# The ninth power in an angular attention kernel: three squarings on ScalarE and one product on VectorE, in place of two squares and two products

## The chip, the cores and the metric

The kernel runs on one core of a Trainium2 chip. The metric is the device time of one execution in microseconds (us). Engines are named as in the profile: PE (TensorE), ACT (ScalarE), DVE (VectorE), POOL (GpSimd), SP (SyncE, which here only starts DMAs).

## The reference, cut to what matters

The program is four residual layers over 4096 tokens of width 128: an angular attention, a mixture of experts, a linear attention, and the mixture of experts again. The change touches the first layer alone:

```
Q = _l2_normalize(x)
K = _l2_normalize(k_weight)
s = jnp.clip(jnp.einsum('nh,ih->ni', Q, K), -1.0 + 1e-06, 1.0 - 1e-06)
B = jnp.power(1.0 - jnp.arccos(s) / jnp.pi, TAU)      # TAU = 9
X = jnp.einsum('ni,ih->nh', B, q_weight)
X = _l2_normalize(X) + bias
```

There are 512 keys, so B has 4096 x 512 values. Up to a factor that the normalisation of X removes, B is the ninth power of (arctan(z) + pi/2), with z = s / sqrt(1 - s^2).

## The kernel before, in words

The program is written engine by engine. Each engine has its own list of instructions, in an order fixed in the code; the engines meet only at semaphores. A helper, `steps(engine, count, unroll, parts)`, writes a software pipeline: each part has a lag, and step s does part(s - lag) for every part in the order given. Where at least two rounds of `unroll` steps fit between the first steps and the last, `steps` turns them into a loop of the engine; else all is written out straight (lines 67 to 94).

The 4096 tokens are 8 groups (NG) of 512. For the scores each group is split in two halves of the keys, so there are 16 units (NA), numbered n; a unit is a tile of 128 x 1024 fp32. First come the scores: PE multiplies (line 815), ACT squares and takes the inverse root (lines 624, 628), DVE multiplies (`tangent`, line 1182) and leaves z of all 16 units in SBUF (`big`). When all are done, ACT loads the table that has the arctangent, and the stage of the ninth power begins. I call it the power stage. For unit n, in slot k = n % 4 of the buffers RR and SC:

- `angle` (ACT, line 647): RR = arctan(z). It waits until `ninth` of unit n - 4 has freed the slot.
- `angle_square` (ACT, line 651): SC = (RR + pi/2)^2.
- `third` (DVE, line 1232): RR = (RR + pi/2) * SC, the third power.
- `sixth` (ACT, line 655): SC = RR^2, the sixth power.
- `ninth` (DVE, line 1239): PB = RR * SC.

After every second unit a group g is whole:

- `value` (PE, line 835): PB times q_weight into the PSUM tile PC, 32 matmuls in the trace. It waits for `ninth`, and for `add_values` of group g - 2, which frees its PC bank.
- `value_squares` (ACT, line 665): four sums of squares of 128 columns, for the norm.
- `x_scale` (POOL, lines 539 and 503): the inverse root of the norm.
- `add_values` (DVE, line 1250): adds the scaled rows to X, and takes the statistics of the next layer norm (line 1036).

On ACT a step is `angle(n)`, `sixth(n-2)`, `angle_square(n)`, and on every second step `value_squares` of the group whose last unit is n - 5. On DVE a step is `ninth(n-3)`, `third(n)`, and on every second step `add_values` for unit n - 7. When all eight groups are in, `statistics(1)` on DVE combines the statistics of all tokens (line 1060 on); no token of the mixture of experts can start before. POOL writes a memset of 7 us (line 548) after its last `x_scale`.

Of the kernel before, what the change touches and what calls it, by code (L numbers as in the profile page):

```python
# [16 lines left out]
ALU = mybir.AluOpType  # L17
ACT = mybir.ActivationFunctionType
# [18 lines left out]
HALF_PI = float(np.pi / 2)  # L37
# [10 lines left out]
def wait(engine, semaphore, value):  # L48

    if isinstance(value, int) and value <= 0:  # L50
        return
    engine.wait_ge(semaphore, value)
# [8 lines left out]
def steps(engine, count, unroll, parts, table=None):  # L61

    most = max(lag for lag, _ in parts)

    first = unroll * (1 + -(-max(0, most - 1) // unroll)) if unroll > 2 else 2 * -(-(most + 1) // 2)
    loops = max(0, (count - first) // unroll)  # L70

    def straight(s):
        for lag, part in parts:
            u = s - lag
            if 0 <= u < count:
                part(u, u // unroll, u % unroll, *(table(u, 1) if table else ()))

    if loops < 2:
        for s in range(count + most):
            straight(s)  # L80
        return
    for s in range(first):
        straight(s)
    with engine.Fori(0, loops) as i:
        known = {}
        for k in range(unroll):
            for lag, part in parts:
                c = (k - lag) % unroll
                h = i + (first + k - lag - c) // unroll
                if table and k - lag not in known:  # L90
                    known[k - lag] = table(i * unroll + (first + k - lag), 1)[0]
                part(h * unroll + c, h, c, *([known[k - lag]] if table else ()))
    for s in range(first + loops * unroll, count + most):
        straight(s)


def build(nc, x_in, ln_w, ln_b, k_w, q_w, a_bias, w_qkv, w_out, gate_w, gate_b,
# [12 lines left out]
    NA = 2 * NG  # L110
# [9 lines left out]
    with ctx:  # L120
        def sb(name, shape, dt=F32):
            return ctx.enter_context(nc.sbuf_tensor(name, shape, dt))

        def sem(name):
            return ctx.enter_context(nc.semaphore(name))
# [54 lines left out]
        PB = sb("PB", [P, 2, HB, GT])  # L180
# [6 lines left out]
        SC, RR = sb("SC", [P, 4, 1024]), sb("RR", [P, 4, 1024])  # L187
# [113 lines left out]
        def read(ring, part, slot, n):  # L301
# [7 lines left out]
            bn_done stat_step var_ready root_ready xn_done  # L309
            yt_a ysq_a norm_a qt_a bias_added  # L310
            s_ready u_ready r_ready
            at_ready sq_ready p3_ready s6_ready p9_ready o_ready ss_ready rx_ready
            xh_ready xl_ready xt_ready gate_ready route_step pm_ready counts_ready places_ready
            gap_ready th_ready routed_out_ready rows_ready
            cb_parts cbt_ready b2_loaded b2_steps scattered0 scattered1 scattered2 scattered3
# [9 lines left out]
        s = {n: sem(n) for n in names}  # L325
# [13 lines left out]
        def angles_done(engine, n, h, k):  # L339

            engine.wait_ge(a_read[k % 2], read("A", "score", k % 2, 2 * h + k // 2))
# [14 lines left out]
        def table_values(engine_type, table, stride):  # L356

            def values(u, n):
                _, found = nc.values_load_multi_w_load_instructions(
                    table[0:1, bass.ds(u, n)], [engine_type], min_val=0, max_val=(E - 1) * stride,  # L360
                    skip_runtime_bounds_check_because="the table's experts are clamped")
                return found
            return values
# [223 lines left out]
        def _(act):  # L587
# [62 lines left out]
                act.wait_ge(s["at_ready"], n + 1)  # L650
                act.activation(SC[:, k, :], RR[:, k, :], ACT.Square, bias=halfpi[:]).then_inc(s["sq_ready"], 1)  # L651

            def sixth(n, h, k):
                act.wait_ge(s["p3_ready"], n + 1)
                act.activation(SC[:, k, :], RR[:, k, :], ACT.Square).then_inc(s["s6_ready"], 1)

            def value_squares(n, h, k):
                if k % 2 == 0:
# [10 lines left out]
            act.wait_ge(s["k_squares"], HB)  # L669
            for n in (NA - 2, NA - 1):  # L670
                angles_done(act, n, n // 4, n % 4)
            for n in range(NA + 5):
                for lag, part in ((0, angle), (2, sixth), (0, angle_square), (5, value_squares)):
                    u = n - lag
                    if 0 <= u < NA:
                        part(u, u // 4, u % 4)
# [350 lines left out]
        def _(dve):  # L1027
# [199 lines left out]

            bias_parts()

            def third(n, h, k):  # L1230
                dve.wait_ge(s["sq_ready"], n + 1)
                dve.scalar_tensor_tensor(RR[:, k, :], RR[:, k, :], HALF_PI, SC[:, k, :], ALU.add,
                                         ALU.mult).then_inc(s["p3_ready"], 1)

            def ninth(n, h, k):
                g, slot = 2 * h + k // 2, k // 2
                dve.wait_ge(s["s6_ready"], n + 1)
                wait(dve, s["o_ready"], g - 1)
                dve.tensor_tensor(PB[:, slot, 2 * (k % 2):2 * (k % 2) + 2, :].rearrange("p b t -> p (b t)"),  # L1239
                                  RR[:, k, :], SC[:, k, :], ALU.mult).then_inc(s["p9_ready"], 1)  # L1240

            def add_values(n, h, k):
                if k % 2 == 0:
# [11 lines left out]
                bn(1, g)  # L1255


            steps(dve, NA, 4, [(3, ninth), (0, third), (7, add_values)])
            statistics(1)

            for layer in range(2):
                sp_ = f"shared{layer}"
                if layer:
                    part = "linear"
# [336 lines left out]
```

## Time and profile before

| what | us |
|---|---|
| median of 3 runs | 924.19 (915.52 to 929.87) |
| profiled execution, device time | 923.3 |
| its span in the trace | 921.4 |
| power stage: ACT's table load to the last statistics on DVE | 110.8 to 182.5 |
| PE busy, whole span | 562.0 (61%) |
| DVE busy | 598.9 (65%) |
| ACT busy | 382.5 (42%) |
| POOL busy | 389.8 (42%) |

All times of single instructions come from the one profiled execution. In the timeline the first column is the start, the second the time until the end; on ACT and DVE the end of an instruction overlaps the start of the next by about a tenth of a microsecond, so the cost of an instruction in a full queue is the distance between two starts, not its length.

### The profile page before, as it was taken

The numbers are of one execution on the slowest core, as the hardware profiler recorded it, in microseconds if no ns is written. First come the engines' busy times: TensorE is split into PE (matmuls) and PEld (weight loads), VectorE is DVE, ScalarE is ACT, GpSimd is POOL, SyncE is SP. The second block draws the span as 40 slices with busy tenths as digits, with TensorE's granted clock in tenths as the row PEclk, the third lists the DMA queues.
The fourth block names the chain that finished last, engine by engine and source line by source line (L and its number), as shares of the span: only waits on it lengthen the run. The fifth ranks groups of instructions, "written<-read, shape, count | busy, mean of one in ns | idle before, by whom it ended". The sixth has DMA issues, their size and how long they took to land.

```text
span 921.4 us, 17336 instructions
## 1 busy us (share of the span) xinstructions
PE 562.0 (61%) x5073; PEld 412.8 (45%) x5074; DVE 598.9 (65%) x1367; ACT 382.5 (42%) x685; POOL 389.8 (42%) x360
## 2 busy tenths in 40 slices
PE   0647546544038698888780488442083998887850
PEld 0223246422025376766660377321052676776640
DVE  5899768785268266766674667782473666666644
ACT  1454898452103254545450244451021454644520
POOL 3096012316748306566572000037476026664650
PEclk9977967955559799999995699765586999999985
DMA  9100000001101523332315000001012223232207
GB/s 288 48 0 0 1 0 1 0 1 37 51 26 51 122 43 76 68 72 68 70 45 194 9 1 1 0 18 53 27 44 76 53 42 80 62 77 61 69 36 279
DMA packets 90830, 51.83 MB, mean 56 GB/s; under 512 B 71482, under 2 KB 79892, under 8 KB 90772
## 3 DMA queue, kind: packets, MB, share of 16 engines
q1 hardware_dynamic: 81556, 32.07, 14.3%
q0 software_dynamic: 9216, 19.02, 6.3%
q8 instruction: 32, 0.52, 0.2%
q14 instruction: 26, 0.21, 0.1%
HBM read 16.28 MB, written 24.30 MB: 44 GB/s over the span
## 4 chain that ended last, share of the span: by engine, by line
PE 42%; DVE 21%; issue 19%; ACT 9%; another core or an unknown queue 3%; DMA 3%; POOL 1%; ACTq 0%; DVEq 0%; SPq 0%; POOLq 0%
PE PC L1016 5%; PE PC L1018 4%; PE PC L1017 4%; PE PA L1000 2%; PE PC L979 2%; PE PA L1002 2%; PE PA L1001 2%; DVE PB L1086 2%; PE PC L981 2%; PE PA L849 2%; PE PC L980 2%; PE PA L815 2%; DMA RR<-expert_results 2%; ACT SC L651 1%
## 5 line engine op out<-in xcount | busy, mean ns | idle before, releaser
L579 POOL DMA_INDIRECT expert_results<-RR,DG x160 | 181.3, 1133 | 188.2 <-DVE RR L1548 148.7
L567 POOL DMA_INDIRECT routed_rows<-big,SLQ x128 | 139.6, 1091 | 196.0 <-DVE SLQ L1409 158.8
L771 ACT ACTIVATE SC<-PA,B1T,scl 128x256 f32<-128x256 f32 x216 | 104.0, 568 | 110.3 <-remote 64.0
L1016 PE MATMUL PC<-W2H,big 128*128 x640 | 124.7, 224 | 14.6 <-issue 8.6
L1017 PE MATMUL PC<-W2H,big 128*128 x640 | 122.9, 222 | 7.0 <-issue 7.0
L1018 PE MATMUL PC<-W2L,big 128*128 x640 | 122.8, 222 | 7.1 <-issue 6.9
L1539 DVE SCALAR_TENSOR_TENSOR big<-SC,scl,big 128x1024 f16<-128x1024 f32 x80 | 102.8, 1285 | 2.8
L1548 DVE SCALAR_TENSOR_TENSOR RR<-PC,scl,DG 128x256 f32<-128x256 f32 x80 | 38.4, 481 | 87.3 <-remote 77.2
L730 ACT ACTIVATE SC<-PA,B1T,scl 128x512 f32<-128x512 f32 x64 | 45.0, 776 | 102.1 <-PE PA L937 45.2
L1016 PEld LDWEIGHTS PC<-W2H,big 128*128 128x128 f16 x640 | 63.1, 99 | 36.6 <-issue 28.4
L1536 DVE TENSOR_SCALAR big<-SC,scl 128x1024 f16<-128x1024 f32 x80 | 61.8, 772 | 12.7 <-ACT SC L771 10.6
L1018 PEld LDWEIGHTS PC<-W2L,big 128*128 128x128 f16 x640 | 63.2, 99 | 12.1 <-issue 10.9
L979 PE MATMUL PC<-W2H,big 128*128 128x128 f16 x256 | 52.0, 234 | 26.2 <-DVE big L1447 17.2
L1017 PEld LDWEIGHTS PC<-W2H,big 128*128 128x128 f16 x640 | 63.7, 100 | 9.0 <-issue 8.5
L771 ACT ACTIVATE SC<-PB,B1T,scl 128x256 f32<-128x256 f32 x104 | 50.4, 569 | 34.2 <-remote 17.3
L1000 PE MATMUL PA<-big,W1H 128*128 128x256 f16 x216 | 60.2, 279 | 3.3 <-issue 3.0
L1002 PE MATMUL PA<-big,W1L 128*128 128x256 f16 x216 | 59.7, 276 | 3.4 <-issue 2.9
L1001 PE MATMUL PA<-big,W1H 128*128 128x256 f16 x216 | 59.8, 277 | 2.0 <-issue 2.0
L835 PE MATMUL PC<-QW,PB 128*128 128x128 f32 x256 | 37.1, 314 | 33.1 <-DVE PB L1239 17.5
L981 PE MATMUL PC<-W2H,big 128*128 128x128 f16 x256 | 51.8, 233 | 8.2 <-issue 8.1
L980 PE MATMUL PC<-W2L,big 128*128 128x128 f16 x256 | 51.8, 233 | 6.7 <-issue 6.7
L835 PEld LDWEIGHTS PC<-QW,PB 128*128 128x128 f32 x256 | 35.6, 227 | 35.3 <-DVE PB L1239 18.5
(245 smaller groups left out, 1358.7 us busy)
## 6 DMA issues: line engine op xcount, KB each, us to landing
RR<-expert_results SPq DMA_DIRECT2D x16, 512.0 KB, 4.6
routed_rows<-big SPq DMA_DIRECT2D x24, 130.0 KB
expert_results<-RR,DG POOLq DMA_INDIRECT x160
X<-n_L_attn_a_hidden_states SPq DMA_DIRECT2D x2, 1024.0 KB, 6.7
big<-in_L_ffn_w SPq DMA_DIRECT2D x1, 2048.0 KB, 8.8
routed_rows<-big,SLQ POOLq DMA_INDIRECT x128
out_x<-X SPq DMA_DIRECT2D x8, 256.0 KB, 5.2
big<-routed_rows SPq DMA_TRANSPOSE x80
```

The source lines that it names most:

```text
L567: pool.indirect_dma_start(routed, bass.IndirectOffsetOnAxis(ap=SLQ[:, slot, t, c:c + 1], axis=0), XHL[:, slot, t, c, :].bitcast(I32), None ...
L579: pool.indirect_dma_start(results, bass.IndirectOffsetOnAxis(ap=DG[:, k, r, 0:1], axis=0), YT[:, k, r, :], None).then_inc(result_stored[k] ...
L771: ins = act.activation(HF[:, k % 3, b * RU:(b + 1) * RU], up_out(k, b), ACT.Gelu, scale=INV1, bias=B1T[:, bass.ds(b1_at + b, 1)])
L835: last = pe.matmul(PC[slot][:, t * D:(t + 1) * D], PB[:, slot, b, t * P:(t + 1) * P], QW[:, b, :], start=(b == 0), stop=(b == HB - 1))
L979: pe.matmul(o, hh, W2H[:, c:c + P], start=(b == 0), stop=False)
L1000: pe.matmul(o, W1H[:, at], xh, start=True, stop=False)
L1001: pe.matmul(o, W1H[:, at], xl, start=False, stop=False)
L1002: last = pe.matmul(o, W1L[:, at], xh, start=False, stop=True)
L1016: pe.matmul(o, hh, W2H[:, at], start=(b == 0), stop=False)
L1017: pe.matmul(o, hl, W2H[:, at], start=False, stop=False)
L1018: last = pe.matmul(o, hh, W2L[:, at], start=False, stop=(b == HB - 1))
L1539: dve.scalar_tensor_tensor(HL3[:, k % 3, :], HF[:, k % 3, 0:HB * RU], SH, HH3[:, k % 3, :], ALU.mult, ALU.subtract).then_inc(s["rhl_ready" ...
```

## The change

The ninth power is built as ((a^2)^2)^2 * a, with a = arctan(z) + pi/2. `third` and `sixth` go. Two squarings in place, `fourth` and `eighth`, come on ACT, and `ninth` takes a and a^8 in one DVE instruction that also adds pi/2. `value_squares` and `add_values` lag by 3 steps and no longer by 5 and 7.

```
-            def sixth(n, h, k):
-                act.wait_ge(s["p3_ready"], n + 1)
-                act.activation(SC[:, k, :], RR[:, k, :], ACT.Square).then_inc(s["s6_ready"], 1)
+            def fourth(n, h, k):
+                act.wait_ge(s["sq_ready"], n + 1)
+                act.activation(SC[:, k, :], SC[:, k, :], ACT.Square).then_inc(s["p4_ready"], 1)
+
+            def eighth(n, h, k):
+                act.wait_ge(s["p4_ready"], n + 1)
+                act.activation(SC[:, k, :], SC[:, k, :], ACT.Square).then_inc(s["p8_ready"], 1)
...
-            for n in range(NA + 5):
-                for lag, part in ((0, angle), (2, sixth), (0, angle_square), (5, value_squares)):
+            for n in range(NA + 3):
+                for lag, part in ((0, angle), (1, fourth), (0, angle_square), (1, eighth), (3, value_squares)):
...
-            def third(n, h, k):
-                dve.wait_ge(s["sq_ready"], n + 1)
-                dve.scalar_tensor_tensor(RR[:, k, :], RR[:, k, :], HALF_PI, SC[:, k, :], ALU.add,
-                                         ALU.mult).then_inc(s["p3_ready"], 1)
-
             def ninth(n, h, k):
                 g, slot = 2 * h + k // 2, k // 2
-                dve.wait_ge(s["s6_ready"], n + 1)
+                dve.wait_ge(s["p8_ready"], n + 1)
                 wait(dve, s["o_ready"], g - 1)
-                dve.tensor_tensor(PB[:, slot, 2 * (k % 2):2 * (k % 2) + 2, :].rearrange("p b t -> p (b t)"),
-                                  RR[:, k, :], SC[:, k, :], ALU.mult).then_inc(s["p9_ready"], 1)
+                dve.scalar_tensor_tensor(PB[:, slot, 2 * (k % 2):2 * (k % 2) + 2, :].rearrange("p b t -> p (b t)"),
+                                         RR[:, k, :], HALF_PI, SC[:, k, :], ALU.add,
+                                         ALU.mult).then_inc(s["p9_ready"], 1)
...
-            steps(dve, NA, 4, [(3, ninth), (0, third), (7, add_values)])
+            steps(dve, NA, 4, [(0, ninth), (3, add_values)])
```

How the order changes. ACT, at the end of the power stage, before: L647 is `angle`, L655 `sixth`, L651 `angle_square`, L665 `value_squares`.

```order
L647 ACTIVATE RR<-big 128x1024
L655 ACTIVATE SC<-RR 128x1024
L651 ACTIVATE SC<-RR,halfpi 128x1024
L665 ACTIVATE junk,SS<-PC 128x128 x4
L647 ACTIVATE RR<-big 128x1024
L655 ACTIVATE SC<-RR 128x1024
L651 ACTIVATE SC<-RR,halfpi 128x1024
L655 ACTIVATE SC<-RR 128x1024
L665 ACTIVATE junk,SS<-PC 128x128 x4
L655 ACTIVATE SC<-RR 128x1024
L665 ACTIVATE junk,SS<-PC 128x128 x8
```

The same place in the changed kernel, where L655 is `fourth`, L659 `eighth`, and L669 `value_squares`:

```order
L647 ACTIVATE RR<-big 128x1024
L655 ACTIVATE SC<-SC 128x1024
L651 ACTIVATE SC<-RR,halfpi 128x1024
L659 ACTIVATE SC<-SC 128x1024
L669 ACTIVATE junk,SS<-PC 128x128 x4
L647 ACTIVATE RR<-big 128x1024
L655 ACTIVATE SC<-SC 128x1024
L651 ACTIVATE SC<-RR,halfpi 128x1024
L659 ACTIVATE SC<-SC 128x1024
L655 ACTIVATE SC<-SC 128x1024
L659 ACTIVATE SC<-SC 128x1024
L669 ACTIVATE junk,SS<-PC 128x128 x8
```

A step has four large passes and no longer three. The last `fourth` and `eighth` stand next to each other, and no `value_squares` is left between the last two units.

DVE, at the end of the power stage, before: L1239 is `ninth`, L1232 `third`, L1250 and L1036 `add_values`.

```order
L1232 SCALAR_TENSOR_TENSOR RR<-RR,SC 128x1024
L1239 TENSOR_TENSOR PB<-RR,SC 128x1024
L1250 SCALAR_TENSOR_TENSOR X<-PC,RX,X 128x128 x4
L1036 BN_STATS BN<-X 128x6 x4
L1239 TENSOR_TENSOR PB<-RR,SC 128x1024 x2
L1250 SCALAR_TENSOR_TENSOR X<-PC,RX,X 128x128 x4
L1036 BN_STATS BN<-X 128x6 x4
```

The same place in the changed kernel: the second half of the loop's body, from the `ninth` (L1238) of its third unit on, and what stands behind the loop (L1250 and L1040 are `add_values`; ISA and REGISTER_ALU rows compute addresses and waits).

```order
L1238 SCALAR_TENSOR_TENSOR PB<-RR,SC 128x1024
L1246 ISA
L1250 ISA
L1250 SCALAR_TENSOR_TENSOR X<-PC,RX,X 128x128
...
L1040 BN_STATS BN<-X 128x6
L1236 REGISTER_ALU
L1238 SCALAR_TENSOR_TENSOR PB<-RR,SC 128x1024
L84 REGISTER_ALU
L84 COMPARE_AND_BRANCH
L1250 SCALAR_TENSOR_TENSOR X<-PC,RX,X 128x128 x4
L1040 BN_STATS BN<-X 128x6 x4
```

DVE's steps 8 to 15 are now a loop of two rounds, which they were not before; the largest lag fell from 7 to 3, and with it the steps that must be written out. In each round, and so in the last one too, an `add_values` stands between the third unit's `ninth` and the fourth's.

## Rows read from the trace of the kernel before

**Rows 1.** The page, part 1: busy time, share of the span, instructions.

```profile
PE 562.0 (61%) x5073; PEld 412.8 (45%) x5074; DVE 598.9 (65%) x1367; ACT 382.5 (42%) x685; POOL 389.8 (42%) x360
```

**Rows 2.** Busy time by stretch: the power stage; all after the next statistics.

```profile
core 0: us, PE busy (x) PEld busy (x) DVE busy (x) ACT busy (x) POOL busy (x), PEclk, DMA share, GB/s
110.80:182.50 71.70, 37.11 (x256) 35.60 (x256) 55.50 (x106) 58.79 (x114) 14.40 (x17) 0.79 0.00 0
189.00:921.40 732.40, 467.04 (x4696) 352.51 (x4696) 447.71 (x1098) 270.63 (x502) 321.08 (x289) 0.82 0.23 60
```

**Rows 3.** Who waited for whom, 110.8 to 182.5: us, times, longest us.

```profile
PE PC L835 <- DVE X L1250: 15.7, 6, 5.9
DVE RR L1232 <- ACT SC L651: 11.2, 13, 1.7
ACT junk L665 <- PE PC L835: 9.3, 5, 3.5
ACT RR L647 <- DVE PB L1239: 1.0, 2, 0.5
```

**Rows 4.** Timeline of ACT, power stage: start, length, instruction [idle before, releaser].

```profile
112.11 1.06 ACT L647 ACTIVATE RR<-big 128x1024 f32<-128x1024 f32 x1
113.20 1.15 ACT L651 ACTIVATE SC<-RR,halfpi 128x1024 f32<-128x1024 f32 x1
114.25 1.04 ACT L647 ACTIVATE RR<-big 128x1024 f32<-128x1024 f32 x1
...
119.31 1.04 ACT L647 ACTIVATE RR<-big 128x1024 f32<-128x1024 f32 x1
120.26 1.04 ACT L655 ACTIVATE SC<-RR 128x1024 f32<-128x1024 f32 x1
121.20 1.13 ACT L651 ACTIVATE SC<-RR,halfpi 128x1024 f32<-128x1024 f32 x1
122.24 1.04 ACT L647 ACTIVATE RR<-big 128x1024 f32<-128x1024 f32 x1
...
131.04 0.26 ACT L665 ACTIVATE junk<-PC 128x128 f32<-128x128 f32 x1
...
132.04 1.06 ACT L647 ACTIVATE RR<-big 128x1024 f32<-128x1024 f32 x1
...
168.75 1.07 ACT L655 ACTIVATE SC<-RR 128x1024 f32<-128x1024 f32 x1
173.27 0.28 ACT L665 ACTIVATE junk<-PC 128x128 f32<-128x128 f32 x1 [3.45 <-PE PC L835]
...
177.58 0.28 ACT L665 ACTIVATE junk<-PC 128x128 f32<-128x128 f32 x1 [3.17 <-PE PC L835]
```

**Rows 5.** Timeline of ACT in the score stage: a pass in place.

```profile
96.71 1.06 ACT L628 ACTIVATE SC<-SC 128x1024 f32<-128x1024 f32 x1
```

**Rows 6.** Timeline of DVE, end of the power stage.

```profile
167.08 1.22 DVE L1239 TENSOR_TENSOR PB<-RR,SC 128x1024 f32<-128x1024 f32 x1
168.22 1.12 DVE L1250 SCALAR_TENSOR_TENSOR X<-PC,RX,X 128x128 f32<-128x128 f32 x4
169.49 0.87 DVE L1036 BATCH_NORM_STATS2 BN<-X 128x6 f32<-128x128 f32 x4
170.27 2.34 DVE L1239 TENSOR_TENSOR PB<-RR,SC 128x1024 f32<-128x1024 f32 x2
...
181.65 0.87 DVE L1036 BATCH_NORM_STATS2 BN<-X 128x6 f32<-128x128 f32 x4
```

**Rows 7.** Timeline of PE, power stage: four of the eight products with q_weight.

```profile
140.37 6.59 PE L835 MATMUL PC<-QW,PB 128*128 128x128 f32 x32 [5.88 <-DVE X L1250]
147.88 3.84 PE L835 MATMUL PC<-QW,PB 128*128 128x128 f32 x32 [0.93 <-DVE X L1250]
156.33 5.47 PE L835 MATMUL PC<-QW,PB 128*128 128x128 f32 x32 [4.62 <-DVE X L1250]
173.71 3.84 PE L835 MATMUL PC<-QW,PB 128*128 128x128 f32 x32 [0.47 <-DVE X L1250]
```

**Rows 8.** Timeline of DVE: statistics in a loop, in the linear attention.

```profile
546.17 0.86 DVE L1036 BATCH_NORM_STATS2 BN<-X  x4
```

**Rows 9.** Groups by line and shape, 110.8 to 182.5: count, busy us, mean ns.

```profile
L1232 DVE SCALAR_TENSOR_TENSOR RR<-RR,SC 128x1024 f32<-128x1024 f32 x16 | 19.6, 1224 | 11.2 <-ACT SC L651 11.2
L1239 DVE TENSOR_TENSOR PB<-RR,SC 128x1024 f32<-128x1024 f32 x16 | 19.4, 1215 | 0.0
```

More of the change, by code:

```diff
@@ L311, in build @@
             s_ready u_ready r_ready
-            at_ready sq_ready p3_ready s6_ready p9_ready o_ready ss_ready rx_ready
+            at_ready sq_ready p4_ready p8_ready p9_ready o_ready ss_ready rx_ready
             xh_ready xl_ready xt_ready gate_ready route_step pm_ready counts_ready places_ready
```

## The prediction

> **What bounds the kernel now.** I read the page first and then asked it only for the place of the change. The page gives DVE as the busiest engine of the compute engines that the change touches, 65% against 42% for ACT [rows 1]. That is a mean over the whole program. The busy time by stretch turns it round for the power stage: in its 71.7 us ACT is busy 58.8 us (82%), DVE 55.5 us (77%), PE 37.1 us [rows 2]. No engine is full, so the waits have to say who holds whom. DVE's `third` waits for ACT in 13 of 16 units, 11.2 us in all; PE waits for `add_values` of DVE in 6 of 8 groups, 15.7 us, since the PC bank comes free late; and ACT waits for that PE in five `value_squares`, 9.3 us, and twice for a slot, 1.0 us [rows 3]. Two of those five waits, 3.45 and 3.17 us, lie behind the last `sixth`, in the drain of the pipeline [rows 4]; so 9.3 - 3.45 - 3.17 + 1.0 = 3.7 us is what ACT loses while it still has large passes to do. The reader is to see: ACT is nearly the bound here, with 3.7 us to spare up to its last pass, and DVE is second.
>
> Outside the stage nothing overlaps it. It begins when all scores are done, and it ends in statistics over all tokens, which everything later needs; no DMA runs in it (share 0.00 [rows 2]). A shift of its end is a shift of the kernel's end, unless later stages happen to run otherwise.
>
> **The change part by part.** I follow ACT from its second `angle` at 114.25 [rows 4], which stands at the same place in both orders (arctangent, square, arctangent), and whose inputs the change doesn't touch.
>
> *One large pass more for each unit on ACT.* The three starts 119.31, 120.26, 121.20, and the next `angle` at 122.24, give 0.95 us for the arctangent, 0.94 for the plain square, 1.04 for the square with the bias from SBUF, 2.93 us for a step [rows 4]. The new step has a second plain square, so 2.93 + 0.95 = 3.88 us. 15 steps (n = 1 to 15) are 58.2 us. Between them lie six `value_squares` (groups 0 to 5) of 132.04 - 131.04 = 1.00 us each, 6.0 us. The last `fourth` starts at 114.25 + 58.2 + 6.0 = 178.45. The last `eighth` stands directly behind it and needs its result; the distance of two such dependent neighbours is 113.20 - 112.11 = 1.09 us [rows 4]. It starts at 179.54 and ends 1.04 us later, at 180.58. Before, the last `sixth` ended at 168.75 + 1.07 = 169.82. So ACT is 10.8 us later. As a check: 16 passes of 0.95 are 15.2 us, less the 3.7 us of waits that vanish is 11.5; the 0.7 us between the two is what the first and the last steps of the old pipeline lost.
>
> Passes in place were not seen in this stage. In the score stage one takes 1.06 us from and to SC [rows 5], the same as a pass between two tiles. Below 0.94 us there is no reason for one. Above, the bound is that each of the 32 shows its result's latency, 1.09 in place of 0.95: 31 x 0.14 = 4.3 us more. I take nothing, since between `angle_square` and `fourth`, and between `fourth` and `eighth`, another pass lies, as lay between `angle` and `angle_square` before, which show 0.94 there.
>
> *DVE loses a pass and gets a loop.* `third` goes, 16 x 1.14 us of queue (168.22 - 167.08 is the distance behind a large product [rows 6]), about 18 us; `ninth` becomes the form of `third`, 1.224 against 1.215 us [rows 9], 0.01 us. None of the 18 us is on ACT's path: it is worth nothing beyond the 3.7 us of waits above. The loop of two rounds adds address and branch work. Statistics inside a loop take 0.86 us for four [rows 8], those written out 0.87 [rows 6], so the body costs nothing that rows show; a round's branch and the first entry are not in a row, and I allow up to 1 us. It is covered: for a group of 2 x 3.88 + 1.00 = 8.76 us DVE has 2 x 1.14 + 1.27 + 0.78 = 4.3 us of work, so 4.4 us are free, except at the very end.
>
> The Trainium skill (ScalarE: Activation LUTs, Rules for kernel authors) says that products belong on VectorE and not on ScalarE, for a speed up to three times higher in bf16. In fp32 the rows here show 1.14 us for a product on DVE and 0.95 us for a square on ACT, so its reason doesn't hold, but its direction does, because ACT is the fuller engine of this stage.
>
> *Who waits for whom in the middle.* From the end of `eighth` of a group's second unit to its `value_squares` ACT does two steps and one other `value_squares`, 8.7 us. In that time fit `ninth` 1.2 us, the matmuls 3.84 us with the clock high up to 6.59 us after a long idle stretch [rows 7], and two hand-overs of 0.05: 5.1 to 7.9 us. There is room, 0.8 us in the worst case, so ACT shouldn't wait. `add_values` needs only `value_squares` of the step before it, and `value` finds its bank free. `angle` waits for a `ninth` three steps back. PE will be idle 8.76 - 3.84 = 4.9 us in each group when fast; in the rows an idle of 4.6 and 5.9 us is followed by 5.47 and 6.59 us of matmuls, one of 0.93 or 0.47 us by 3.84 [rows 7]. So PE will be slower here, unseen.
>
> *The drain.* Two things stand ahead of the last product. The last-but-one `ninth` starts when its `eighth` ends, at 178.45 + 0.10 = 178.55. Behind it DVE has `add_values` of group 5 and only then the last `ninth`: 1.14 + 1.27 + 0.78 = 3.19 us [rows 6], so 181.74, which is 1.2 us later than the last `eighth` would allow. It ends at 182.96 and PE starts at 183.0. Then come the last 32 matmuls. Bounds are 3.84 and 6.59 us; PE will have been idle for about 8.0 less its own burst, 1.5 to 4.2 us, between the idles of the fast and the slow rows, so I take the middle, 5.2 us. From the end of the matmuls to the last statistics took (181.65 + 0.87) - (173.71 + 3.84) = 4.97 us [rows 6, 7], and the same instructions stand there. Sum: 183.0 + 5.2 + 4.97 = 193.2, against 182.5 before: **10.7 us later**. Of these, ACT is 10.8, the wait of the drain 183.0 - 180.58 against 173.71 - 169.82 is -1.5, and the slower matmuls are +1.4. With both bounds of the matmuls: 9.3 to 12.1 us.
>
> The profiled execution took 923.3 us for a span of 921.4. 923.3 + 10.7 = 934.0 us. It lay 0.9 us under the median of the runs shown, well inside their 14 us, so I leave it there.
>
> **The rivals.**
>
> *Dependent passes show their latency.* The queue of ACT now has three passes of each unit that hang on one another. If each costs 1.09 us, the 4.3 us above come on top: 938.3. For it speaks the pair at 112.11 and 113.20; against it that `angle_square` two places behind its `angle` shows nothing.
>
> *ACT stalls for PE in every group.* If the matmuls stay slow in all groups and DVE's loop delays `ninth`, the 7.9 us of the chain pass the 8.7 us of cover. It decides from 0.8 us of delay on, and each further 1 us costs 1 us in each of 7 groups. With the allowance of 1 us for the loop in each round and matmuls of twice 3.84 = 7.7 us (not seen in a row) the chain is 10.0 us, 1.3 too long, 7 x 1.3 = 9 us more: 943. Against it: the loop has only two rounds.
>
> *The other side: DVE is the bound, and the change is no loss.* The page shows DVE fullest [rows 1], the ring of PC banks runs over DVE's queue, and the change takes 18 us from it and shortens the lags. If ACT's passes could be packed more closely than 0.95 us the ring would set the pace; it would gain the 3.7 us, and the drain 1.5 more: 923.3 - 5.2 = 918. Its condition is that the 16 new passes (15.2 us) cost less than 15.2 - 10.7 = 4.5 us, 0.28 us each. A square of 1024 columns at 0.94 us in 16 rows speaks plainly against it. The Trainium skill (Perfetto Trace Analysis, Identifying the Most-Contended Engine, and Optimizing Scalar/DVE Operations) says to relieve the engine with the highest occupancy first, and that work moved from a saturated DVE to ScalarE may help; it also says to look within a regime. The occupancy of the whole span supports this rival, that of the stage doesn't.
>
> *The loss is given back later.* From 189 us on the clock of PE is 0.82 on the mean [rows 2]; between levels of 0.5 and 1.0 this is 36% of 732 us, 264 us, at the low one. A shifted start changes what falls into them. To win back 10.7 us, 21 us of these 264 would have to turn fast on the chain. That is 924 or less. The spread of the runs before, 14 us, says that such sizes occur, in both directions.
>
> **How the numbers follow.** Chances: the forecast 0.62, latency of dependent passes 0.13, stalls in every group 0.07, given back later 0.14, DVE as the bound 0.04. The forecast's own range with the bounds of matmuls and loop and half of the runs' spread is 928 to 940. The full range takes in the latency rival and most of the give-back: 923 to 943. About 2% (18.5 us) is what a measurement of this kernel can tell from no change; the forecast, 1.1% slower, lies within. Slower by over 2% needs the stalls or two rivals together, 0.08; faster by over 2% needs the DVE rival and more, 0.02; within 2% 0.90.
>
> **What would show it.** ACT's starts in the stage should be 0.95 apart with no idle ahead of `value_squares` up to the last `eighth`, which ends near 180.6. DVE's busy time in the stage falls by some 19 us and it waits for `eighth` in nearly every unit. The last `ninth` starts 1.2 us after the last `eighth` ended, behind `add_values`. Matmuls of a group take 4 to 6.6 us. The last statistics end near 193, and all behind it is shifted by that. The prediction is wrong if plain squares in place are 1.09 apart, if ACT waits for PE ahead of `value_squares`, or if the stage is 10 us longer and the kernel isn't.

## The result, and where the time went

| | median us | runs |
|---|---|---|
| kernel before | 922.43 | 4 (915.52 to 929.87) |
| changed kernel | 944.24 | 4 (942.88 to 949.85) |

The ratio is 1.0235 with a 95% interval of 1.018 to 1.029: 21.8 us slower, twice the 10.7 us that were forecast, and 1.2 us outside the range. I compare the profiled execution (944.69 us, span 942.5) with that of before (923.3 and 921.4).

The timeline of ACT in the changed kernel, at the start of the power stage, in a middle step and at the end:

```profile
111.53 1.06 ACT L647 ACTIVATE RR<-big 128x1024 f32<-128x1024 f32 x1
112.62 1.15 ACT L651 ACTIVATE SC<-RR,halfpi 128x1024 f32<-128x1024 f32 x1
113.67 1.04 ACT L647 ACTIVATE RR<-big 128x1024 f32<-128x1024 f32 x1
114.62 1.04 ACT L655 ACTIVATE SC<-SC 128x1024 f32<-128x1024 f32 x1
115.56 1.13 ACT L651 ACTIVATE SC<-RR,halfpi 128x1024 f32<-128x1024 f32 x1
116.60 1.04 ACT L659 ACTIVATE SC<-SC 128x1024 f32<-128x1024 f32 x1
117.55 1.04 ACT L647 ACTIVATE RR<-big 128x1024 f32<-128x1024 f32 x1
...
177.82 1.12 ACT L655 ACTIVATE SC<-SC 128x1024 f32<-128x1024 f32 x1
178.97 1.06 ACT L659 ACTIVATE SC<-SC 128x1024 f32<-128x1024 f32 x1
...
186.54 0.28 ACT L669 ACTIVATE junk<-PC 128x128 f32<-128x128 f32 x1 [5.40 <-PE PC L839]
```

These answer to [rows 4]. The step is 117.55 - 113.67 = 3.88 us, as worked out. The squares in place stand 0.94 and 0.95 us before the next start. There is no bracket with idle time between the first pass and the last: ACT is full. The last `eighth` ends at 180.03, 68.5 us after the first arctangent; before it was 169.82 - 112.11 = 57.7. ACT is 10.8 us later, the number of the forecast.

The timeline of DVE over the drain:

```profile
178.03 1.23 DVE L1238 SCALAR_TENSOR_TENSOR PB<-RR,SC 128x1024 f32<-128x1024 f32 x1 [3.66 <-ACT SC L659]
179.17 1.12 DVE L1250 SCALAR_TENSOR_TENSOR X<-PC,RX,X 128x128 f32 x4
180.54 0.87 DVE L1040 BATCH_NORM_STATS2 BN<-X  x4 [0.25 <-DVE X L1250]
181.33 1.21 DVE L1238 SCALAR_TENSOR_TENSOR PB<-RR,SC 128x1024 f32<-128x1024 f32 x1
...
190.60 0.87 DVE L1040 BATCH_NORM_STATS2 BN<-X 128x6 f32<-128x128 f32 x4
```

The last `ninth` starts at 181.33, 1.3 us after its input was there, behind `add_values` of group 5; the same pieces before are in [rows 6]. The timeline of PE, against [rows 7]:

```profile
156.97 5.70 PE L839 MATMUL PC<-QW,PB 128*128 128x128 f32 x32 [4.94 <-DVE PB L1238]
165.73 3.83 PE L839 MATMUL PC<-QW,PB 128*128 128x128 f32 x32 [3.06 <-DVE PB L1238]
174.50 5.46 PE L839 MATMUL PC<-QW,PB 128*128 128x128 f32 x32 [4.94 <-DVE PB L1238]
182.67 3.83 PE L839 MATMUL PC<-QW,PB 128*128 128x128 f32 x32 [2.71 <-DVE PB L1238]
```

All eight starts hang on `ninth`, none on the PC bank any more. The last product took 3.83 us, the lower bound. The busy time by stretch says the same of the whole stage, against [rows 2]:

```profile
110.20:191.47 81.27, 38.12 (x256) 36.62 (x256) 37.50 (x90) 73.25 (x130) 13.29 (x17) 0.79 0.00 0
```

(Columns: stretch, its length, busy us of PE, PE's weight loads, DVE, ACT, POOL, the granted clock.) DVE fell from 55.5 to 37.5 us, ACT rose from 58.8 to 73.3. From the first arctangent to the first statistics over all tokens the stage took 79.98 us against 70.44: 9.5 us longer.

So a little under half of the loss lies here and the rest does not. With the last product at its lower bound, the forecast for the stage was 9.3 us.

I divide what is left at the first DVE operation behind the root (R), the first load of routed rows (X0, X1), the first load of results (Y0, Y1), and the first statistics behind the linear attention (M):

| us | before | changed |
|---|---|---|
| R to X0: gates, shared expert, scatter, layer 0 | 131.4 | 137.6 |
| X0 to Y0: routed experts | 172.8 | 173.4 |
| Y0 to M: linear attention | 93.7 | 93.7 |
| M to X1: gates, shared expert, layer 1 | 131.7 | 140.8 |
| X1 to Y1 | 182.5 | 178.0 |
| Y1 to end | 20.2 | 21.0 |
| R to end | 732.3 | 744.5 |

12.2 us more. The two stages with the shared expert, whose code the change doesn't touch, are 6.2 and 9.1 us longer, 15.3 in all, and the second pass of the routed experts is 4.5 us shorter. What PE shows there: one line of the shared expert's product (L980 before, L984 in the changed kernel), its durations and what it waited for, in layer 0. First before:

```profile
L980 PE MATMUL PC<-W2L,big x128: 216/219/314, 268.7 to 335.3; 128*128 128x128 f16 x128
  issue: 5.7, 8
```

and the changed kernel:

```profile
L984 PE MATMUL PC<-W2L,big x128: 216/219/314, 277.7 to 351.5; 128*128 128x128 f16 x128
  issue: 7.8, 11
```

(Shortest, median and longest duration in ns, first and last start.) The product starts as late behind R in both, 79.6 and 79.7 us, and in layer 1 as late behind M, 81.9 and 82.2 us. So the stages grow behind its start: up to X0 from 51.8 to 57.8 us, up to X1 from 49.8 to 58.7. The same 128 matmuls spread over 73.8 us in place of 66.6. PE sits idle for "issue", which is time in which nothing that the profile shows holds it. In the changed kernel the timeline has it in pieces of half a microsecond, ahead of single matmuls:

```profile
290.86 0.22 PE L985 MATMUL PC<-W2H,big 128*128 128x128 f16 x1 [0.39 <-issue]
291.61 0.22 PE L984 MATMUL PC<-W2L,big 128*128 128x128 f16 x1 [0.47 <-issue]
292.32 0.23 PE L985 MATMUL PC<-W2H,big 128*128 128x128 f16 x1 [0.50 <-issue]
```

The mean granted clock is lower too: over the stretch of the shared expert 0.78 before (259 to 320 us) and 0.70 in the changed kernel (268 to 335 us). Which of the two comes first isn't shown. Such idle time stands in both kernels, and on this line it is only 2.1 us more in the changed one, which is less than the 7.2 us of the spread. Did the change cause this?

### The profile page after: what moved, and what is told of

Read it like the earlier page. It is cut to its first block, busy times and chain, and to the rows that moved or that the text cites. A ratio compares the mean times of both kernels' runs of the same rounds, so it can differ in the third digit from the quotient of the medians.

```text
span 942.5 us, 17389 instructions
## 1 busy us (share of the span) xinstructions
PE 571.8 (61%) x5073; PEld 419.7 (45%) x5074; DVE 580.7 (62%) x1351; ACT 397.3 (42%) x701; POOL 387.9 (41%) x360
## 4 chain that ended last, share of the span: by engine, by line
PE 41%; DVE 20%; issue 19%; ACT 12%; another core or an unknown queue 3%; DMA 3%; POOL 1%; DVEq 0%; SPq 0%; ACTq 0%; POOLq 0%
PE PC L1020 5%; PE PC L1022 4%; PE PC L1021 4%; PE PC L983 2%; PE PA L1004 2%; PE PA L1006 2%; PE PA L1005 2%; PE PC L985 2%; DVE PB L1090 2%; PE PC L984 2%; PE PA L853 2%; DMA RR<-expert_results 2%; ACT RR L647 2%; ACT SC L659 2%
## 5 line engine op out<-in xcount | busy, mean ns | idle before, releaser
L579 POOL DMA_INDIRECT expert_results<-RR,DG x160 | 183.9, 1150 | 200.0 <-DVE RR L1548 162.7
L567 POOL DMA_INDIRECT routed_rows<-big,SLQ x128 | 136.2, 1064 | 196.4 <-DVE SLQ L1409 159.2
L1020 PE MATMUL PC<-W2H,big 128*128 x640 | 127.3, 227 | 15.4 <-issue 10.8
L1022 PE MATMUL PC<-W2L,big 128*128 x640 | 125.3, 225 | 9.2 <-issue 9.2
L1021 PE MATMUL PC<-W2H,big 128*128 x640 | 125.9, 225 | 5.1 <-issue 4.9
L1020 PEld LDWEIGHTS PC<-W2H,big 128*128 128x128 f16 x640 | 64.0, 100 | 38.8 <-issue 30.7
L1021 PEld LDWEIGHTS PC<-W2H,big 128*128 128x128 f16 x640 | 64.8, 101 | 10.0 <-issue 9.5
L983 PE MATMUL PC<-W2H,big 128*128 128x128 f16 x256 | 53.4, 238 | 24.5 <-DVE big L1447 17.2
L839 PE MATMUL PC<-QW,PB 128*128 128x128 f32 x256 | 38.1, 319 | 41.7 <-DVE PB L1238 41.7
L985 PE MATMUL PC<-W2H,big 128*128 128x128 f16 x256 | 53.4, 238 | 8.9 <-issue 8.9
L984 PE MATMUL PC<-W2L,big 128*128 128x128 f16 x256 | 53.4, 237 | 8.6 <-issue 8.6
```

The lines of the kernel that those rows point to most:

```text
L567: pool.indirect_dma_start(routed, bass.IndirectOffsetOnAxis(ap=SLQ[:, slot, t, c:c + 1], axis=0), XHL[:, slot, t, c, :].bitcast(I32), None ...
L579: pool.indirect_dma_start(results, bass.IndirectOffsetOnAxis(ap=DG[:, k, r, 0:1], axis=0), YT[:, k, r, :], None).then_inc(result_stored[k] ...
L839: last = pe.matmul(PC[slot][:, t * D:(t + 1) * D], PB[:, slot, b, t * P:(t + 1) * P], QW[:, b, :], start=(b == 0), stop=(b == HB - 1))
L983: pe.matmul(o, hh, W2H[:, c:c + P], start=(b == 0), stop=False)
L1020: pe.matmul(o, hh, W2H[:, at], start=(b == 0), stop=False)
L1021: pe.matmul(o, hl, W2H[:, at], start=False, stop=False)
```

## The experiments

Theory SHIFT: the shared stages take a later start badly, by 12 us. Theory CODE or LOOP: the changed instruction lists do it, above all DVE's new loop. The third possibility is that it belonged to that measurement and not to the change. Fifteen runs were made in four sets, each on another chip (1, 7, 5 and 3) and beside the kernel before. The sets lie at different levels: the kernel before took 909.3, 912.7, 819.9 and 820.6 us. Whether a level belongs to the chip or to the occasion can't be told from them, and the chip of the first measurement is not on record. So times are compared within a set.

### Set 1: delay, loop, one pass fewer

**e1_shift9** puts nine chained passes on ACT ahead of the root of the next layer norm:

```
+                for i in range(passes):      # 9 in layer 0
+                    act.activation(SC[:, 0, :], SC[:, 0, :], ACT.Square, scale=1e-6).then_inc(s["spent"], 1)
+                    act.wait_ge(s["spent"], i + 1)
                 act.activation(EST[:], VA[:], ACT.Abs_reciprocal_sqrt).then_inc(s["root_ready"], 1)
```

> The kernel before, with nine squarings of a 128x1024 tile in a chain on ACT between the last variance and the root of the next layer norm: a pure delay of 9 x 1.09 = 9.8 us behind the power stage, the size of what the change adds ahead of it (9.5 us). Nothing else moves. Theory SHIFT (the 12 us that the change loses behind the stage come from when the experts' stages start against the clock's windows or the DMAs): the kernel loses about 9.8 + 12 = 22 us, 945. Theory CODE (they come from the changed code, DVE's new loop or the places where instruction fetches fall): it loses 9.8 us, 932.

Measured: 1.0148 (1.0094 to 1.0202), 13.5 us. The first statistics to the next root took 17.6 us and not 6.6: the delay is 11.0 us. The nine passes are 9.8 of it; the rest is a table load of 1.28 us on ACT, which now stands behind them. SHIFT wanted twice that; the interval, 8.5 to 18.4 us, holds the delay alone and excludes 22.

**e2_no_loop** writes DVE's part of the changed kernel out:

```
-            steps(dve, NA, 4, [(0, ninth), (3, add_values)])
+            for n in range(NA + 3):
+                for lag, part in ((0, ninth), (3, add_values)):
+                    u = n - lag
+                    if 0 <= u < NA:
+                        part(u, u // 4, u % 4)
```

> The changed kernel with DVE's ninth and add_values written out straight, as they stood before, and no loop. Theory LOOP (the new loop on DVE causes the 12 us behind the stage): about 932. Theory SHIFT: 944, as the changed kernel. Theory CODE in its wide form (where instruction fetches fall): between, since DVE's list is longer by some 20 instructions.

Measured: 1.0147 (1.01 to 1.0195), 13.4 us: between what LOOP and SHIFT wanted. Taken against the first measurement it spoke for LOOP, but the two come from different sets; e6 and e8 below compare them on one chip.

**e3_no_fourth** drops `fourth` (DVE then multiplies by a^4, so the output is the fifth power's):

```
-                for lag, part in ((0, angle), (1, fourth), (0, angle_square), (1, eighth), (3, value_squares)):
+                for lag, part in ((0, angle), (0, angle_square), (1, eighth), (3, value_squares)):
```

> The changed kernel without the fourth power: ninth multiplies by a^4, and the output is another one. ACT is back at three large passes a unit. The stage should shorten by 16 x 0.95 = 15.2 us plus the changed hand-overs, to about 66 us, 6 us shorter than before the change. Theory SHIFT: what lies behind the stage is that of before or otherwise, unlike the changed kernel's; 917 or so if it is that of before. Theory LOOP or CODE: the 12 us behind the stage stay, 929.

Measured: 1.0004 (0.9969 to 1.004). The stage took 70.3 us, not 66. My expectation forgot two things that the trace shows. First, `angle_square` now stands directly behind its `angle`:

```profile
146.01 1.04 ACT L647 ACTIVATE RR<-big 128x1024 f32<-128x1024 f32 x1
147.09 1.15 ACT L651 ACTIVATE SC<-RR,halfpi 128x1024 f32<-128x1024 f32 x1
148.14 1.04 ACT L655 ACTIVATE SC<-SC 128x1024 f32<-128x1024 f32 x1
```

1.08 and 1.05 us to the next start in place of 0.95 and 1.04. Second, with shorter steps ACT waits for PE again (0.60, 1.12 and 0.31 us ahead of three `value_squares` before the drain), and the drain stays as long as in the changed kernel. Still the run says one thing clearly: one pass a unit, 16 x 0.95 = 15.2 us of ACT, is the difference between the changed kernel and no loss, although its DVE has the loop and the 18 us of relief.

**e4_before_loop** gives the kernel before a DVE loop of two rounds, by one more argument of `steps`:

```
-            steps(dve, NA, 4, [(3, ninth), (0, third), (7, add_values)])
+            steps(dve, NA, 4, [(3, ninth), (0, third), (7, add_values)], first=8)
```

> The kernel before, with DVE's power stage as a loop of two rounds instead of written out; the same instructions in the same order. Theory LOOP: the stage keeps its length and the kernel loses 12 us behind it, 935. Theory SHIFT: no change, 922 to 924.

Measured: 0.9982 (0.9932 to 1.0032), the stage 70.5 us. The upper end of the interval is 3 us, far from LOOP's 12: a loop on DVE costs nothing that shows. LOOP is out, as far as the loop alone goes.

### Set 2: the changed kernel again, and a tighter pipeline

**e6_changed_again** is the changed kernel, **e7_before_traced** the kernel before, **e8_straight_again** the kernel of e2.

> The changed kernel itself, once more, beside the kernel before and the next runs. The straight version and the pure delay of nine passes each lost 1.5%, about 13 us, where the changed kernel was measured at 2.35%. If the changed kernel's extra is real and comes from DVE's loop: ratio 1.023 again. If it belonged to that measurement (the chip, or how the experts' stages fell): ratio 1.012 to 1.017, some 11 to 15 us, with the stage 9 to 12 us longer and nothing systematic behind it.

> The kernel before, unchanged, with a trace beside those of the other runs of this set. The ratio is 1.00. Its time from the root of the second layer norm to the end was 732.3 us in the first trace; SHIFT wants about 720 in this set, clearly less than in the changed kernel; the other theory wants the same length as in all the others of the set, give or take 5 us.

> The changed kernel without DVE's loop, beside the one with it. LOOP: 8 us faster than the changed kernel. Otherwise: the same within 0.5%.

Measured: the changed kernel 1.0119 (1.008 to 1.0157) over 6 runs against 23 of before, 923.03 against 912.69 us; the kernel before 0.9973 (0.994 to 1.0005); the straight version 1.0138 (1.0095 to 1.018). The loss of the changed kernel is 10.9 us here, and its interval does not touch that of the first measurement. Loop and no loop are the same. From R to the end the traces of sets 1 and 2 show 717.6 to 727.1 us in the seven runs other than e7, in no order of the start of R; e7 has 713.4. With R near 188 to 189 us (e3, e4, e7, e9) the mean is 719.7; with R at 197.6 to 200.5 us (e1, e2, e6, e8) it is 721.2. No effect of a late start of 12 us is in this.

**e9_tight** keeps the passes of the kernel before and shortens the lags:

```
-                for lag, part in ((0, angle), (2, sixth), (0, angle_square), (5, value_squares)):
+                for lag, part in ((0, angle), (2, sixth), (0, angle_square), (4, value_squares)):
...
-            steps(dve, NA, 4, [(3, ninth), (0, third), (7, add_values)])
+            steps(dve, NA, 4, [(2, ninth), (0, third), (5, add_values)])
```

> The passes of the kernel before (three on ACT, two on DVE), with ninth at lag 2, value_squares at lag 4 and add_values at lag 5 in place of 3, 5 and 7. ACT's waits (3.7 us) and one step of the drain go; the stage ends about 6 us earlier, near 176.5, and the kernel takes 6 us less than before (ratio 0.993). If what lies behind the stage depends on when it starts, the time can come out up to 10 us to either side of that.

Measured: 0.9994 (0.9966 to 1.0022); a miss. The stage took 70.2 us. The timeline of PE at the end:

```profile
159.12 3.83 PE L835 MATMUL PC<-QW,PB 128*128 128x128 f32 x32 [1.60 <-DVE PB L1239]
166.51 10.18 PE L835 MATMUL PC<-QW,PB 128*128 128x128 f32 x64 [3.55 <-DVE PB L1239]
```

The product of group 6 started at 166.51, behind a `ninth` that had itself stood behind `add_values` on DVE, and after 3.55 us of idle it and the last product took 10.2 us together. The step that failed is that ACT's 3.7 us of waits would go: up to its last `sixth` ACT still waited 3.2 us, 1.13, 0.72 and 0.38 us for PE ahead of three `value_squares` and 1.01 us for `third`. Why is argued and not tested: a group is 4 x 1.14 + 2.05 = 6.6 us of work on DVE and 6.9 us on ACT, so either engine is nearly full, and taking out one wait brings the next.

### Set 3: ACT's pass alone, and the order in the drain

**e10_fourth_pass** gives the kernel before a fourth large pass on ACT, a copy in place, and leaves DVE as it was:

```
+            def again(n, h, k):
+                act.wait_ge(s["spent"], n + 1)
+                act.activation(SC[:, k, :], SC[:, k, :], ACT.Copy).then_inc(s["s6_ready"], 1)
...
+                for lag, part in ((0, angle), (2, sixth), (0, angle_square), (2, again), (5, value_squares)):
```

> The kernel before with one more pass of 128x1024 on ACT for each unit, a copy of the sixth power onto itself behind angle_square; DVE keeps third and ninth. If ACT's pass alone makes the loss and DVE's relief is worth nothing: ACT's steps 3.88 us, the last large pass ends 10 to 11 us later than before, the stage is 9 to 12 us longer, the ratio 1.010 to 1.015, as the changed kernel. If DVE's relief gives something back in the changed kernel, this one is slower than the changed kernel by that, up to 3 us in the stage.

> The changed kernel a third time, for the ratio and for the spread behind the stage. By the chain worked out for the power stage: ratio 1.012 (1.008 to 1.016). If the first measurement's 1.0235 was the rule and the second the exception: 1.02 or more.

> The changed kernel with add_values ahead of ninth in DVE's steps, so that add_values of group 5 fills DVE's idle time before the last-but-one ninth and no longer stands between the last two. The last ninth starts when the last eighth ends, 1.1 us earlier against it than in the changed kernel (there 1.2 us behind the end of eighth), and the stage is 1.2 us shorter; in the time 0.1%, which can't be told.

> The kernel before, with a trace beside those of this set: power stage 70.5 us from the first arctangent to the statistics, and a time from the root of the layer norm to the end within 8 us of that of the changed kernel's in this set.

Measured: e10 1.0135 (1.0112 to 1.0157), e11 (the changed kernel) 1.0105 (1.0081 to 1.0129), e12 1.0092 (1.0064 to 1.012). e13 was a single execution. Traces: the stage took 70.2 us in e13 (before), 80.1 in e10 and 81.4 in e11. The last product of e10, then of e11:

```profile
182.51 3.84 PE L839 MATMUL PC<-QW,PB 128*128 128x128 f32 x32 [1.17 <-DVE X L1254]
```

```profile
182.72 5.25 PE L839 MATMUL PC<-QW,PB 128*128 128x128 f32 x32 [2.71 <-DVE PB L1238]
```

At equal products the two stages are alike within 0.1 us. **ACT's pass alone lengthens the stage by 9.9 us, as much as the changed kernel's is longer at equal products, and in the order that it has, the changed kernel gets nothing of it back for a DVE without `third` and with shorter lags.** The drains differ in kind, though: e10's last product waits 1.1 us behind its `ninth` for `add_values` to free the bank, and the changed kernel's last `ninth` waits 1.3 us behind `add_values`. By the medians e10 takes 2.2 us more than e11 (830.71 and 828.53; their intervals overlap). Its traced stage is not the longer one; the traces have the difference behind it, 631.1 against 629.0 us from R to the end.

e12 swaps two parts of the changed kernel:

```
-            steps(dve, NA, 4, [(0, ninth), (3, add_values)])
+            steps(dve, NA, 4, [(3, add_values), (0, ninth)])
```

Its ACT and DVE at the end:

```profile
178.62 1.06 ACT L659 ACTIVATE SC<-SC 128x1024 f32<-128x1024 f32 x1
```

```profile
177.72 1.21 DVE L1238 SCALAR_TENSOR_TENSOR PB<-RR,SC 128x1024 f32<-128x1024 f32 x1
179.71 1.22 DVE L1238 SCALAR_TENSOR_TENSOR PB<-RR,SC 128x1024 f32<-128x1024 f32 x1 [0.78 <-ACT SC L659]
```

The last `ninth` now starts 0.03 us after the last `eighth` ends (179.68). The stage is 78.7 us; against e11's 81.4, 1.4 of the 2.7 us are the product (3.83 against 5.25), and 1.3 the swap. The stage is also 1.4 us shorter than e10's, at equal products. By these single traces the changed kernel can get a little back in the drain, once DVE's order allows it; which part of that is the missing `third` and which the shorter lags is not shown. In the time it can't be told, as expected.

### Set 4: once more, against the pure delay

> The changed kernel once more. If this set's kernel before takes 915 to 930 us, as in the first measurement: a ratio of 1.02 or more says that the 12 us behind the power stage belong to the change in that condition, 1.008 to 1.016 that they were how its four runs fell. In a set of another level: 1.008 to 1.016.

> The kernel before with the pure delay of nine passes ahead of the root, 11 us measured. If what lies behind the stage takes a late start badly in this set, this one loses as much as the changed kernel, twice its delay; else 1.2 to 1.5%.

> The kernel before with its trace beside them: the length from the root to the end, and of the experts' stages in it, to hold against the changed kernel's. Without an effect of the change behind the stage the two agree within the 10 us that they scattered in the second set.

Measured: the changed kernel 1.0103 (1.0084 to 1.0121), 828.91 against 820.63 us; the pure delay 1.0143 (1.0128 to 1.0159); before 1.0001. R to end: 629.4, 629.4 and 631.1 us; in set 3 631.1 (e10), 629.0 (e11), 626.2 (e12) and 631.0 (e13). Here nothing behind the stage depends on the change or on the delay, within 5 us. In sets 3 and 4 the changed kernel's traced stage is 11.2 and 11.4 us longer, more than the loss in time of 8.6 and 8.5 us; the profiled executions (830.69 and 831.12 us) lay 2.2 us above their medians, and R to the end was 2.0 and 1.7 us shorter than before.

In these two sets the idle time on issue is gone. The same line as above, in layer 0, first e13 (before), then e11 (changed); neither answer has an issue row:

```profile
L980 PE MATMUL PC<-W2L,big x128: 219/219/314, 239.4 to 296.3; 128*128 128x128 f16 x128
```

```profile
L984 PE MATMUL PC<-W2L,big x128: 219/219/314, 250.9 to 309.0; 128*128 128x128 f16 x128
```

57 and 58 us, against 66.6 and 73.8 in the first measurement, and in set 2, e7 (before):

```profile
L980 PE MATMUL PC<-W2L,big x128: 216/219/314, 258.3 to 335.6; 128*128 128x128 f16 x128
  issue: 10.1, 10
```

77 us. Between e7 and e13, both the kernel before, R to X0 differs by 21 us (140.5 and 119.2) and X0 to Y0 by 25 us (161.6 and 137.1): the levels of the sets lie in the experts' stages. The first measurement's excess lay there too.

Yet no later set came back at its condition. The routed experts of layer 0 took 172.8 us there, 159 to 167 in sets 1 and 2, 136 to 137 in sets 3 and 4. The gates, which choose the experts of each token ahead of the shared expert's product, show it as well. DVE writes their choice (`PM`, line 1365) 69.9 us behind R in both first traces, 47 to 50 us behind it in all eight traces of sets 1 and 2, and 41.7 us in all seven of sets 3 and 4. Line 1361 on the way there had DVE idle on issue for 18.1 us (before) and 19.0 us (changed) in the first traces, for 3.9 us in e7, and not at all in e13. So DVE, too, stood still without a shown cause.

I lean to the view that the excess belonged to that condition and not to the change. That is argued, and one thing speaks against plain scatter: the first interval (1.018 to 1.029) lies above those of all three repeats (at most 1.0157). An effect of the delay, or of where the instructions fall in their lists, that shows in that condition alone is not excluded. Whether the change costs 12 us more there stays open.

## Why the prediction was right or wrong

- **What bounds the stage: right.** ACT was nearly the bound with 3.7 us to spare, and became it. DVE's waits for `eighth` (37.2 us) and ACT's single wait, in the drain, show it.
- **One pass more on ACT: right.** Step 3.88 us forecast and measured; last pass 10.8 us later forecast and measured. e10 isolates it.
- **Passes in place: right** at 0.94 us. The rival of dependent passes is out: only the two pairs of dependent neighbours show it, the first (111.53 to 112.62, 1.09 us) and the last (177.82 to 178.97, 1.15 us).
- **DVE's relief is worth nothing: right for the stage as written** (e10 against e11). DVE's busy time fell by 18.0 us, where some 19 were forecast. The rival with DVE as the bound had the page's 65% for it and is out: the stage got longer with 18 us less on DVE.
- **The loop on DVE: right** (e4, e8). Its price is at most 0.25 us of idle in an `add_values`.
- **Stalls in every group: out.** ACT didn't wait once before the drain, even with products of 6.7 us in e6 (165.48 to 172.22).
- **The drain: right.** The 1.2 us behind `add_values` are there, and e12 removes them. The last product was put at 5.2 us, by how long PE would have been idle. It took 3.83, 5.17, 5.25 and 5.46 us in four traces of the changed kernel (e6, e11 and e14 are the later ones), each time after 2.71 us of idle. In the straight version it took 6.79 us in e2, above the upper bound of 6.59, and 3.83 in e8, each after 2.60. So the idle time does not tell the duration, and where 5.2 came near, it was luck. The stage came out 9.5 us longer in the first trace, and 10.4, 11.2 and 11.4 us in the later ones (e6 against e7, e11 against e13, e14 against e16), for a forecast of 10.7.
- **Where it failed:** "A shift of its end is a shift of the kernel's end, unless later stages happen to run otherwise." I took what later stages might do as half of the runs' spread, 7 us, but the range of 928 to 940 has no room for it: 6 us above 934 less 1.4 for the matmuls and 1 for the loop is 3.6. And I gave a chance only to a gain ("the loss is given back later"), none to a loss of the same size. In the first measurement the later stages ran 12.2 us longer: 6.2 and 9.1 us in the two shared-expert stages, less 4.5 us in the second pass of the routed experts. Why they did stays open. The spread of 14 us between three runs of one kernel said that this could happen. In the three later sets the changed kernel was 1.19%, 1.05% and 1.03% slower, by the ratios 10.9, 8.6 and 8.5 us, where the forecast had 10.7 us on 923, 1.16%.

For the power stage the mechanism and the size hold, and by the three later sets so does the loss of the kernel. In the first measurement half of the loss came from stages for which the forecast had no term.

## What to carry to other kernels

Read the busy shares of the stretch that a change touches, not those of the page: here the busiest engine of the whole run was the second in the stage, and work taken from it gave nothing back, while each of the sixteen passes added to the other cost 0.95 us. Count the slack of the engine that gets the work (3.7 us here) against what is added (15.2 us); the difference, 11.5 us, is the loss to within a microsecond (10.8 at ACT's last pass). And where a kernel's own runs scatter by 14 us, widen the range by that on both sides, and measure a 1% change in more than one set before explaining the second percent.

## What the runs showed of the hardware

- The same kernel took 922, 909 to 913, and 820 us in different measurements, with nearly equal times in the power stage (70.2 to 70.9 us) and in the linear attention (93.6 to 93.9 us), and 131.4, 140.5 and 119 us from R to X0. In the sets at 909 us and above PE idled on issue ahead of single matmuls of the shared expert; in those at 820 us it never did on that line in layer 0. The amount of it does not follow the level: 5.7 us of it on that line at 922 us (before), 10.1 us at 913 (e7).
- Two neighbouring ACT passes of 128x1024 of which the second reads the first's result start 1.07 to 1.16 us apart (1.07 to 1.11 in e3, 1.09 on the mean in the nine passes of e1, 1.16 in e12). Where another pass lies between the two, each pass is followed by its neighbour after 0.94 to 0.97 us, or 1.03 us and more if it reads a bias from SBUF.
- Products of 32 fp32 matmuls that came every 8.8 us alternated, in the first trace, between 3.83 us and 5.5 to 5.9 us; in e6 and e11 seven of eight took 5.2 to 6.7. The mean clock of the stage was 0.79 in the first trace, as before the change.
